# Four residual buffers instead of two, and a layernorm product written in place, in an eight-core random-feature and gated-FFN kernel

## The chip, the cores and the metric

The kernel runs on the 8 cores of one Trainium2 chip. Every core runs the same program on its own 2048 tokens, and nothing passes between the cores. The metric is the device time of one execution, in microseconds (us), taken on the slowest core. The profile is of core 1.

## The reference

For x of shape (4, 4096, 1024), 16384 tokens of width 1024:

```python
xn = _layernorm(x)
s = rfs_attention(xn)          # feats(xn) @ weights.T, both from exp(dot - correction)
h = silu(xn @ w1.T * w1_s) * (xn @ w2.T * w2_s)        # 1024 -> 4096
h = gelu(h @ h1.T * h1_s)                               # 4096 -> 4096
h = gelu(h @ h2.T * h2_s)                               # 4096 -> 4096
g = silu(h @ w3.T * w3_s)                               # 4096 -> 1024
x = x + s * g
```

## The kernel before

Each core works through its 2048 tokens in four sweeps of 512 (`for s_ in range(NS)`, L385). Activations lie feature-major: a tile of 128 features by 512 tokens is one matmul's moving operand. In a sweep TensorE (PE) does, in this order: `ffn1_strip` for 8 strips (L390 to L443: w1 at L401, w2 at L424), the layernorm broadcast of the next sweep (L273, L275), the two 4096 by 4096 layers h1 and h2 (L484), `emit_dot0` of the next sweep (L357), the w3 layer in two halves of four output tiles (L514), and `emit_smm` of the next sweep (L374). Sweep 0 does its own dot and smm product early; so there are three sweep boundaries at which the w3 half is followed directly by `emit_smm`, and one end of the program without it.

Weights come through `wring`, a ring of five slots of 1 MB in bf16 (2 MB in HBM, cast in flight), loaded by `ring_load` (L216, L222) on GpSimd's queue. A load waits until PE has used up the slot's last contents.

The residual part (L539 to L565) ends a sweep. The w3 output goes from PSUM through a Silu on ScalarE (L527) into `t2`, VectorE (DVE) multiplies it into `s_sb` (L534), adds x (L556, x being loaded by `xt_load` into a slot of `xt_r`), and SyncE (SP) stores `s_sb[:, dc, :]` to y (L562). There are eight tiles dc of 128 features in a sweep. `xt_r` has two slots, so the load of tile dc + 2 is issued only when the add of tile dc has freed its slot:

```python
for dc in range(8):
    slot = dc % 2
    ...
    av = V(... tensor_add(s_sb[:, dc, :], xt_r[:, slot, :], s_sb[:, dc, :]))
    if dc + 2 < 8:
        xt_load(dc + 2)
    need(sy, cV, av)
    sy.dma_start(y[...], s_sb[:, dc, :])
```

Waits are semaphore waits placed by `need`. Every engine runs its own program in the order in which the code emits it; no scheduler reorders it. What matters at a sweep boundary: `emit_smm` makes eight output tiles in PSUM banks 0 to 3, `oc % 4`. Its tiles 0 to 3 find their banks free. Tile 4 needs bank 0 again, so it waits for DVE to copy tile 0 into `s_sb` (L379). On DVE that copy is emitted behind the eight adds of L556. The copy also waits until the y store of the same `s_sb` tile has landed (`need(v, d_y[oc], ...)`, L378).

`ln2_bcast_affine` (L269 to L286) makes the normalised activations: for each of eight tiles a product into the fp32 tile `ln_tmp` (L280) and a subtraction into the bf16 tile `xn_fm` (L281), with the two PSUM banks 4 and 5 as second operands. In sweeps 1 to 3 it runs while PE is in h1; in sweep 0 PE waits for its last instruction (L282) before the first `emit_dot0`. Instructions of DVE are chained one behind the other by `V`, which waits for the instruction before.

Of the kernel before, what the change touches and what calls it, by code (L numbers as in the profile page):

```python
# [7 lines left out]
F32 = mybir.dt.float32  # L8
# [7 lines left out]
TS = 512  # L16
# [21 lines left out]
def build_nc():  # L38
    nc = bass.Bass("TRN2", target_bir_lowering=False)
    g = nc.gpsimd  # L40
    sy = nc.sync
    t = nc.tensor
    v = nc.vector
    sc = nc.scalar

    xT = nc.dram_tensor("xT", [D, T], F32, kind="ExternalInput").ap()
# [17 lines left out]
    with contextlib.ExitStack() as stack:  # L64
        E = stack.enter_context

        def sb(name, shape, dtype):
            return E(nc.sbuf_tensor(name, shape, dtype))
# [1 line left out]
        projT_sb = sb("projT_sb", [128, 9, R], BF16)  # L70
        Wt_sb = sb("Wt_sb", [128, 8, R], BF16)
        xt_sweep = sb("xt_sweep", [128, 8, TS], BF16)
        xt_r = sb("xt_r", [128, 2, 512], F32)
        rows = sb("rows", [128, 4, TS], F32)
        ln_tmp = sb("ln_tmp", [128, TS], F32)
        xn_fm = sb("xn_fm", [128, 9, TS], BF16)
        feats = sb("feats", [128, 8, TS], BF16)
        s_sb = sb("s_sb", [128, 8, TS], F32)
# [26 lines left out]
        p = [E(nc.psum_tensor(f"pb{i}", [128, 512], F32)) for i in range(8)]  # L105

        cT = Ctr(nc, stack, "cT", t)
        cV = Ctr(nc, stack, "cV", v)
        cS = Ctr(nc, stack, "cS", sc)
        d_xts = Ctr(nc, stack, "d_xts", g)  # L110
        d_xt = [Ctr(nc, stack, f"d_xt{i}", sy) for i in range(2)]
        d_y = [Ctr(nc, stack, f"d_y{i}", sy) for i in range(8)]
        d_wr = [Ctr(nc, stack, f"d_wr{i}", g) for i in range(5)]
        d_ident = Ctr(nc, stack, "d_ident", sy)
# [6 lines left out]
        def need(eng, ctr, val, allow_self=False):  # L121
            if ctr is None or val <= 0:
                return
            if ctr.eng is eng and not allow_self:
                return
            key = (id(eng), id(ctr.sem))
            if waited.get(key, 0) >= val:
                return
            eng.wait_ge(ctr.sem, val)
            waited[key] = val  # L130
# [3 lines left out]
        def guard_bank(i):  # L134
            gd = bank_guard.get(i)
            if gd is not None:
                need(t, gd[0], gd[1])

        def V(instr_fn):
            need(v, cV, cV.n, allow_self=True)  # L140
            return cV.inc(instr_fn())
# [74 lines left out]
        def ring_load(nm, strip, kk8, first):  # L216
            nonlocal ring_seq
            slot = ring_seq % 5
            fsrc = srcs[nm][strip] if nm in ("w1", "w2") \
                else srcs[nm][strip][:, kk8 * 8:(kk8 + 1) * 8, :]  # L220
            need(g, cT, slot_last[slot])
            g.dma_start(wring[:, slot, :, :], fsrc).then_inc(d_wr[slot].sem, 16)  # L222
            d_wr[slot].n += 16
            ring_seq += 1
            return slot, d_wr[slot], d_wr[slot].n
# [43 lines left out]
        def ln2_bcast_affine(s_, ffn1_last):  # L269
            need(t, cV, ln_state["rows"])  # L270
            guard_bank(4)
            guard_bank(5)
            bc1 = cT.inc(t.matmul(p[4][:, :], ones_row[0:1, :], rows[0:1, 2, :],  # L273
                                  start=True, stop=True))
            bc2 = cT.inc(t.matmul(p[5][:, :], ones_row[0:1, :], rows[0:1, 3, :],  # L275
                                  start=True, stop=True))
            need(v, cT, bc2)
            need(v, cT, ffn1_last)
            for j in range(8):
                V(lambda j=j: v.tensor_mul(ln_tmp[:, :], xt_sweep[:, j, :], p[4][:, :]))  # L280
                V(lambda j=j: v.tensor_sub(xn_fm[:, j, :], ln_tmp[:, :], p[5][:, :]))  # L281
            xr = V(lambda: v.tensor_copy(xn_fm[0:1, 8, :], rows[0:1, 1, :]))  # L282
            bank_guard[4] = (cV, xr)
            bank_guard[5] = (cV, xr)
            xts_state["guard"] = xr
            return xr  # L286
# [5 lines left out]
        xt_guard = {}  # L292
# [51 lines left out]
        ln2_stats(0)  # L344
        emit_wphase()
        xn_ready_sweep = ln2_bcast_affine(0, 0)

        def emit_dot0(xn_rdy):
            need(t, cast_sem["projT"], 16)
            need(t, cast_sem["xisrow"], 16)  # L350
            need(t, cV, xn_rdy)
            need(t, cV, cols_ready)
            for rc in range(8):
                bk = (6, 7, 4, 5)[rc % 4]
                guard_bank(bk)
                for j in range(9):
                    ii = t.matmul(p[bk][:, :], projT_sb[:, j, rc * 128:(rc + 1) * 128],  # L357
                                  xn_fm[:, j, :], start=(j == 0), stop=(j == 8))
                stop = cT.inc(ii)
                need(sc, cT, stop)  # L360
                ev = S(lambda rc=rc, bk=bk: sc.activation(
                    feats[:, rc, :], p[bk][:, :], AF.Exp,
                    bias=bias_f[:, rc:rc + 1], scale=ab_col[:, rc:rc + 1]))
                bank_guard[bk] = (cS, ev)
            return cS.n
# [19 lines left out]
        for s_ in range(NS):  # L385
            tok0 = s_ * TS
# [78 lines left out]
            if s_ + 1 < NS:  # L465
                xn_ready_sweep = ln2_bcast_affine(s_ + 1, ffn1_last)
# [3 lines left out]
            for nm, src_sb, dst_sb, s_col, src_rdy, dst_rec in (  # L470
# [3 lines left out]
                for ss in range(8):  # L474
# [3 lines left out]
                    for kk in range(4):  # L478
                        need(t, rdy_ctr, rdy_map[2 * kk + 1])
                        slot, wc, wv = ring_load(nm, ss, kk, s_ == 0)  # L480
# [19 lines left out]
            if s_ + 1 < NS:  # L500
                feats_next = emit_dot0(xn_ready_sweep)

            sg_done = [0] * 8
            for ss in range(2):
                quad = [0, 1, 2, 3] if ss == 0 else [4, 5, 2, 3]
# [2 lines left out]
                for kk in range(4):  # L508
                    need(t, cS, g2_by_strip[2 * kk + 1])
                    slot, wc, wv = ring_load("w3", ss, kk, s_ == 0)  # L510
# [11 lines left out]
                for og in range(4):  # L522
                    dc = ss * 4 + og
# [7 lines left out]
                for og in range(4):  # L531
                    dc = ss * 4 + og
# [3 lines left out]
                    t2_guard[og] = mv  # L536
                    sg_done[dc] = mv

            xt_val = {}  # L539

            def xt_load(dc):
                slot = dc % 2
                need(sy, cV, xt_guard.get(slot, 0))
                sy.dma_start(xt_r[:, slot, :],
                             xT[dc * 128:(dc + 1) * 128, tok0:tok0 + TS])\
                    .then_inc(d_xt[slot].sem, 16)
                d_xt[slot].n += 16
                xt_val[dc] = d_xt[slot].n

            xt_load(0)  # L550
            xt_load(1)
            for dc in range(8):
                slot = dc % 2
                need(v, cV, sg_done[dc])
                need(v, d_xt[slot], xt_val[dc])
                av = V(lambda dc=dc, slot=slot: v.tensor_add(  # L556
                    s_sb[:, dc, :], xt_r[:, slot, :], s_sb[:, dc, :]))
                xt_guard[slot] = av
                if dc + 2 < 8:
                    xt_load(dc + 2)  # L560
                need(sy, cV, av)
                sy.dma_start(y[dc * 128:(dc + 1) * 128, tok0:tok0 + TS],  # L562
                             s_sb[:, dc, :]).then_inc(d_y[dc].sem, 16)
                d_y[dc].n += 16
                y_val[dc] = d_y[dc].n  # L565
# [53 lines left out]
if __name__ == "__main__":  # L619
    nc = build_nc()  # L620
    print("built ok, instructions:", nc.n_instructions())
```

## Time and profile before

| what | value |
| --- | --- |
| median of 2 runs | 2897.07 us (2819.28 and 2974.87) |
| time of the profiled execution | 2818.11 us |
| its span, core 1 (first to last instruction) | 2816.4 us; the eight cores 2810.4 to 2816.4 |
| PE busy | 2636.4 us, 94% of the span |
| DVE, ACT, POOL busy | 251.3, 354.4, 205.3 us |
| mean granted TensorE clock | 0.976 |
| moved by DMA | 396.25 MB, mean 141 GB/s |

The profiled execution's own time is 1.7 us above its span. A row of the timeline is: start in us, duration in us, engine, line, operation, output<-input, count, and in brackets the idle time before it with what ended it. SPq is the SP engine's DMA issue. q0 is GpSimd's DMA queue (software), q1 is SP's (hardware). Idle time of an engine costs only where it delays the engine that sets the end.

### The profile page before, as it was taken

Reading aid. Unit: us, or ns where it says so; the run is one execution under the profiler, and the core shown is the slowest. Engines: PE = TensorE matmul, PEld = TensorE weight load, DVE = VectorE, ACT = ScalarE, POOL = GpSimd, SP = SyncE. Lnnn points to the kernel's source line nnn. Section 1 sums busy time; section 2 is a strip of 40 time slices with the busy share of each in tenths; the row PEclk is TensorE's granted clock in tenths of the full one; section 3 lists DMA queues with packets and bytes.
Section 4 is the critical chain, followed back from the end, with each engine's and each line's share of the span. In section 5 each row is a group of like instructions: output and inputs, shape, how many; then the busy total and the mean of one; then the engine's idle time right before and its main releaser. Section 6 shows DMA issues by size and latency. Waiting matters only on the chain.

```text
span 2816.4 us, 28223 instructions; the slowest of 8 cores (2810.4 to 2816.4 us)
## 1 busy us (share of the span) xinstructions
PE 2636.4 (94%) x12054; PEld 1184.5 (42%) x12054; DVE 251.3 (9%) x382; ACT 354.4 (13%) x493; POOL 205.3 (7%) x391
## 2 busy tenths in 40 slices
PE   2799999999879999999978999999987999999995
PEld 1344444444334444444433444444433444444442
DVE  2123000000022200000012310000002210000001
ACT  0211101010212110101101201010120110101100
POOL 1010000000000000000001000000000000000000
PEclk9899999999989999999998999999998999999997
DMA  9088888888569888888586988888865898888883
GB/s 157 2 137 139 156 152 151 153 154 153 94 134 164 148 151 151 152 153 154 107 141 121 158 152 153 154 153 150 151 117 121 148 153 153 155 153 151 152 154 75
DMA packets 67115, 396.25 MB, mean 141 GB/s; under 512 B 7328, under 2 KB 11696, under 8 KB 21936
## 3 DMA queue, kind: packets, MB, share of 16 engines
q0 software_dynamic: 57408, 377.51, 76.2%
q1 hardware_dynamic: 9584, 16.92, 2.3%
q8 instruction: 98, 1.61, 0.2%
q14 instruction: 25, 0.20, 0.0%
HBM read 763.51 MB, written 8.39 MB: 274 GB/s over the span
## 4 chain that ended last, share of the span: by engine, by line
PE 93%; DMA 3%; DVE 2%; ACT 1%; issue 1%; SPq 0%; DVEq 0%; POOL 0%; ACTq 0%
PE pb L484 63%; PE pb L514 8%; PE pb L401 8%; PE pb L424 8%; PE pb L357 2%; DMA xt_r<-xT 2%; PE pb L374 2%; DMA xt_sweep<-xT 1%; PE pb L333 1%; ACT t L527 0%; DVE s_sb L534 0%; DVE s_sb L556 0%; PE pb L243 0%; PE pb L245 0%; ACT h_sb L495 0%
## 5 line engine op out<-in xcount | busy, mean ns | idle before, releaser
L484 PE MATMUL pb<-h_sb,wring 128*128 128x512 bf16 x4096 | 884.7, 379 | 0.0
L484 PE MATMUL pb<-g_sb,wring 128*128 128x512 bf16 x4096 | 884.7, 379 | 0.0
L484 PEld LDWEIGHTS pb<-h_sb,wring 128*128 128x128 bf16 x4096 | 400.5, 98 | 484.8 <-issue 2.3
L484 PEld LDWEIGHTS pb<-g_sb,wring 128*128 128x128 bf16 x4096 | 400.8, 98 | 483.3
L514 PE MATMUL pb<-h_sb,wring 128*128 128x512 bf16 x1024 | 232.6, 391 | 18.8 <-ACT t L527 18.8
L401 PE MATMUL pb<-xn_fm,wring 128*128 128x512 bf16 x1024 | 231.5, 379 | 0.0
L424 PE MATMUL pb<-xn_fm,wring 128*128 128x512 bf16 x1024 | 231.4, 379 | 0.0
L534 DVE TENSOR_TENSOR s_sb<-t,s_sb 128x512 f32<-128x512 bf16 x32 | 22.2, 692 | 2028.2 <-ACT t L527 2025.4
L495 ACT ACTIVATE h_sb<-pb,h2s_c 128x512 bf16<-128x512 f32 x128 | 87.9, 687 | 795.8 <-PE pb L484 787.0
L495 ACT ACTIVATE g_sb<-pb,h1s_c 128x512 bf16<-128x512 f32 x128 | 87.9, 687 | 692.9 <-PE pb L484 683.7
L514 PEld LDWEIGHTS pb<-h_sb,wring 128*128 128x128 bf16 x1024 | 102.3, 100 | 148.4 <-issue 34.4
L424 PEld LDWEIGHTS pb<-xn_fm,wring 128*128 128x128 bf16 x1024 | 100.2, 98 | 120.8
L401 PEld LDWEIGHTS pb<-xn_fm,wring 128*128 128x128 bf16 x1024 | 99.9, 98 | 121.5 <-issue 1.3
L415 ACT ACTIVATE t<-pb,w1s_c 128x512 bf16<-128x512 f32 x128 | 87.9, 687 | 420.8 <-PE pb L401 414.8
L222 POOL DMA_DIRECT2D wring<-h1p x128 | 67.5, 528 | 827.6 <-PE pb L484 686.0
L222 POOL DMA_DIRECT2D wring<-h2p x128 | 67.5, 527 | 816.5 <-PE pb L484 816.5
L438 DVE SCALAR_TENSOR_TENSOR h_sb<-pb,w2s_c,t 128x512 bf16<-128x512 f32 x128 | 96.0, 750 | 336.5 <-PE pb L424 325.8
L374 PE MATMUL pb<-feats,Wt_sb 128*128 128x512 bf16 x256 | 64.2, 416 | 55.5 <-DVE s_sb L379 55.5
L357 PE MATMUL pb<-xn_fm,projT_sb 128*128 128x512 bf16 x288 | 66.8, 396 | 21.0 <-DVE xn_fm L282 13.4
L374 PEld LDWEIGHTS pb<-feats,Wt_sb 128*128 128x128 bf16 x256 | 26.7, 105 | 92.4 <-issue 67.4
L222 POOL DMA_DIRECT2D wring<-w2p x32 | 17.1, 535 | 530.7 <-PE pb L401 457.6
L357 PEld LDWEIGHTS pb<-xn_fm,projT_sb 128*128 128x128 bf16 x288 | 28.8, 101 | 59.4 <-issue 28.7
(71 smaller groups left out, 380.5 us busy)
## 6 DMA issues: line engine op xcount, KB each, us to landing
wring<-h1p POOLq DMA_DIRECT2D x128, 1024.0 KB, 8.2
wring<-h2p POOLq DMA_DIRECT2D x128, 1024.0 KB, 8.1
wring<-w1p POOLq DMA_DIRECT2D x32, 1024.0 KB, 11.9
wring<-w2p POOLq DMA_DIRECT2D x32, 1024.0 KB, 9.6
wring<-w3p POOLq DMA_DIRECT2D x32, 1024.0 KB, 8.0
xt_r<-xT SPq DMA_DIRECT2D x32, 256.0 KB, 4.6
y<-s_sb SPq DMA_DIRECT2D x32, 256.0 KB, 4.6
xt_sweep<-xT POOLq DMA_DIRECT2D x32, 128.0 KB, 11.8
```

The costliest lines, as they stand in the source:

```text
L222: g.dma_start(wring[:, slot, :, :], fsrc).then_inc(d_wr[slot].sem, 16)
L333: ii = t.matmul(p[bk][:, :], projT_sb[:, j, rc * 128:(rc + 1) * 128], iw_c[j][:, oh * 512:(oh + 1) * 512], start=(j == 0), stop=(j == 8))
L357: ii = t.matmul(p[bk][:, :], projT_sb[:, j, rc * 128:(rc + 1) * 128], xn_fm[:, j, :], start=(j == 0), stop=(j == 8))
L374: ii = t.matmul(p[bk][:, :], Wt_sb[:, rc, oc * 128:(oc + 1) * 128], feats[:, rc, :], start=(rc == 0), stop=(rc == 7))
L401: ii = t.matmul(p[ba1 + og][:, :], wring[:, slot1, k, (hh * 2 + og) * 128:(hh * 2 + og + 1) * 128], xn_fm[:, k, :], start=(k == 0), stop=( ...
L415: ev = S(lambda sl=sl, og=og, oc=oc, ba1=ba1: sc.activation(t1[:, sl, :], p[ba1 + og][:, :], AF.Silu, scale=w1s_c[:, oc:oc + 1]))
L424: ii = t.matmul(p[ba2 + og][:, :], wring[:, slot2, k, (hh * 2 + og) * 128:(hh * 2 + og + 1) * 128], xn_fm[:, k, :], start=(k == 0), stop=( ...
L438: ev = V(lambda oc=oc, og=og, sl=sl, ba2=ba2: v.scalar_tensor_tensor(h_sb[:, oc, :], p[ba2 + og][:, :], w2s_c[:, oc:oc + 1], t1[:, sl, :], ...
L484: ii = t.matmul(p[quad[og]][:, :], wring[:, slot, k8, og * 128:(og + 1) * 128], src_sb[:, kk * 8 + k8, :], start=(kk == 0 and k8 == 0), st ...
L495: sc.activation(dst_sb[:, oc, :], p[quad[og]][:, :], AF.Gelu, scale=s_col[:, oc:oc + 1]))
L514: ii = t.matmul(p[quad[og]][:, :], wring[:, slot, k8, og * 128:(og + 1) * 128], h_sb[:, kk * 8 + k8, :], start=(kk == 0 and k8 == 0), stop ...
L534: mv = V(lambda og=og, dc=dc: v.tensor_mul(s_sb[:, dc, :], t2[:, og, :], s_sb[:, dc, :]))
```

## The change

`xt_r` gets four slots instead of two, each with its own semaphore counter, and the load of tile dc + 4 follows the add of tile dc. The definition of `xt_load` and the first loads (now four) move up in the code, from behind the w3 layer to ahead of it. The fp32 tile `ln_tmp` (2 KB per partition) goes; the product of the layernorm is written as bf16 into its place in `xn_fm`, and the subtraction reads and writes it there. `xt_r` grows by 4 KB per partition.

```diff
-        xt_r = sb("xt_r", [128, 2, 512], F32)
+        xt_r = sb("xt_r", [128, 4, 512], F32)
         rows = sb("rows", [128, 4, TS], F32)
-        ln_tmp = sb("ln_tmp", [128, TS], F32)
...
-        d_xt = [Ctr(nc, stack, f"d_xt{i}", sy) for i in range(2)]
+        d_xt = [Ctr(nc, stack, f"d_xt{i}", sy) for i in range(4)]
...
             for j in range(8):
-                V(lambda j=j: v.tensor_mul(ln_tmp[:, :], xt_sweep[:, j, :], p[4][:, :]))
-                V(lambda j=j: v.tensor_sub(xn_fm[:, j, :], ln_tmp[:, :], p[5][:, :]))
+                V(lambda j=j: v.tensor_mul(xn_fm[:, j, :], xt_sweep[:, j, :], p[4][:, :]))
+                V(lambda j=j: v.tensor_sub(xn_fm[:, j, :], xn_fm[:, j, :], p[5][:, :]))
...
                 feats_next = emit_dot0(xn_ready_sweep)
 
+            xt_val = {}
+
+            def xt_load(dc):
+                slot = dc % 4
...
+            for dc in range(4):
+                xt_load(dc)
+
             sg_done = [0] * 8
...
-            xt_load(0)
-            xt_load(1)
             for dc in range(8):
-                slot = dc % 2
+                slot = dc % 4
                 need(v, cV, sg_done[dc])
                 need(v, d_xt[slot], xt_val[dc])
...
-                if dc + 2 < 8:
-                    xt_load(dc + 2)
+                if dc + 4 < 8:
+                    xt_load(dc + 4)
```

On PE, ScalarE, VectorE and GpSimd the instructions stand in the same order as before. SP's order changes. At the start of its program, before, behind the six small vector loads (`vec_sb`):

```order
L192 DMA vec_sb<-w3s 8x128
L544 DMA xt_r<-xT 128x512 x2
L544 DMA xt_r<-xT 128x512 [waits cV]
L562 DMA y<-s_sb 128x512
L544 DMA xt_r<-xT 128x512 [waits cV]
L562 DMA y<-s_sb 128x512
```

The same place now, where the loads' line is L507:

```order
L191 DMA vec_sb<-w3s 8x128
L507 DMA xt_r<-xT 128x512 x4
L507 DMA xt_r<-xT 128x512 [waits cV]
L562 DMA y<-s_sb 128x512
L507 DMA xt_r<-xT 128x512 [waits cV]
L562 DMA y<-s_sb 128x512
```

Two more loads are issued without a wait at the program's start. At the boundary of two sweeps SP's order before, where `cV` is DVE's counter, that is, the wait for an add:

```order
L544 DMA xt_r<-xT 128x512 [waits cV]
L562 DMA y<-s_sb 128x512
L544 DMA xt_r<-xT 128x512 [waits cV]
L562 DMA y<-s_sb 128x512
L562 DMA y<-s_sb 128x512 [waits cV] x2
L544 DMA xt_r<-xT 128x512 x2
L544 DMA xt_r<-xT 128x512 [waits cV]
L562 DMA y<-s_sb 128x512
```

And now:

```order
L507 DMA xt_r<-xT 128x512 [waits cV]
L562 DMA y<-s_sb 128x512
L507 DMA xt_r<-xT 128x512 [waits cV]
L562 DMA y<-s_sb 128x512
L562 DMA y<-s_sb 128x512 [waits cV] x4
L507 DMA xt_r<-xT 128x512 x4
L507 DMA xt_r<-xT 128x512 [waits cV]
L562 DMA y<-s_sb 128x512
```

In both kernels the first loads of a sweep stand directly behind the last y store of the sweep before, with no wait of their own; there are four of them now, and four loads instead of six that wait for an add.

## Rows read from the trace of the kernel before

**Rows 1.** The page, busy us of each engine (share of span) xinstructions.

```profile
PE 2636.4 (94%) x12054; PEld 1184.5 (42%) x12054; DVE 251.3 (9%) x382; ACT 354.4 (13%) x493; POOL 205.3 (7%) x391
```

**Rows 2.** Who waited for whom: us in total, times, longest us.

```profile
DVE s_sb L556 <- DMA xt_r<-xT: 58.2, 24, 7.2
PE pb L374 <- DVE s_sb L379: 57.3, 3, 20.3
...
PE pb L357 <- DVE xn_fm L282: 13.4, 1, 13.4
...
PE pb L424 <- DMA wring<-w2p: 0.9, 1, 0.9
```

**Rows 3.** Timeline of the first sweep boundary, 786 to 811 us.

```profile
786.46 0.53 POOL L222 DMA_DIRECT2D wring<-w1p  x1 [6.37 <-PE pb L514]
...
790.17 1.49 DVE L556 TENSOR_TENSOR s_sb<-xt_r,s_sb 128x512 f32<-128x512 f32 x2
790.95 0.33 SPq L544 DMA_DIRECT2D xt_r<-xT  x1
...
792.47 0.81 SPq L562 DMA_DIRECT2D y<-s_sb  x1
798.86 0.69 DVE L556 TENSOR_TENSOR s_sb<-xt_r,s_sb 128x512 f32<-128x512 f32 x1 [7.20 <-DMA xt_r<-xT]
...
800.12 0.69 DVE L556 TENSOR_TENSOR s_sb<-xt_r,s_sb 128x512 f32<-128x512 f32 x1 [0.57 <-DMA xt_r<-xT]
...
809.18 0.69 DVE L556 TENSOR_TENSOR s_sb<-xt_r,s_sb 128x512 f32<-128x512 f32 x1 [0.58 <-DMA xt_r<-xT]
...
810.81 9.41 PE L374 MATMUL pb<-feats,Wt_sb 128*128 128x512 bf16 x32 [17.99 <-DVE s_sb L379]
```

**Rows 4.** Timeline of the second sweep boundary: adds of tiles 3 and 7.

```profile
1475.20 0.69 DVE L556 TENSOR_TENSOR s_sb<-xt_r,s_sb 128x512 f32<-128x512 f32 x1 [0.64 <-DMA xt_r<-xT]
...
1487.21 0.69 DVE L556 TENSOR_TENSOR s_sb<-xt_r,s_sb 128x512 f32<-128x512 f32 x1 [1.78 <-DMA xt_r<-xT]
```

**Rows 5.** Timeline of the third sweep boundary: adds of tiles 3 and 7.

```profile
2154.75 0.69 DVE L556 TENSOR_TENSOR s_sb<-xt_r,s_sb 128x512 f32<-128x512 f32 x1 [0.64 <-DMA xt_r<-xT]
...
2165.49 0.69 DVE L556 TENSOR_TENSOR s_sb<-xt_r,s_sb 128x512 f32<-128x512 f32 x1 [2.41 <-DMA xt_r<-xT]
```

**Rows 6.** Timeline of the program's end: adds of tiles 3 and 7.

```profile
2800.72 0.69 DVE L556 TENSOR_TENSOR s_sb<-xt_r,s_sb 128x512 f32<-128x512 f32 x1 [0.47 <-DMA xt_r<-xT]
...
2812.14 0.69 DVE L556 TENSOR_TENSOR s_sb<-xt_r,s_sb 128x512 f32<-128x512 f32 x1 [2.37 <-DMA xt_r<-xT]
```

**Rows 7.** DMA queues, 791 to 796 us: packets, MB, share of 16 engines.

```profile
q0 software_dynamic: 92, 0.69, 90.6%
q1 hardware_dynamic: 21, 0.04, 11.0%
```

**Rows 8.** The same for 796 to 800 us.

```profile
q1 hardware_dynamic: 551, 1.00, 72.9%
```

**Rows 9.** Windows, 796 to 800 us; the last three: granted clock, DMA share, GB/s.

```profile
796.00:800.00 4.00, 0.00 (x0) 0.00 (x0) 0.69 (x1) 0.00 (x0) 0.00 (x0) 0.50 0.76 254
```

**Rows 10.** The page, DMA issues: count, KB each, median us to landing.

```profile
xt_r<-xT SPq DMA_DIRECT2D x32, 256.0 KB, 4.6
```

**Rows 11.** Groups of instructions by form: busy us, mean ns of one.

```profile
L438 DVE SCALAR_TENSOR_TENSOR h_sb<-pb,w2s_c,t 128x512 bf16<-128x512 f32 x128 | 96.0, 750 | 337.5 <-PE pb L424 326.7 <-ACT t L415 4.1
...
L280 DVE TENSOR_TENSOR ln_tmp<-xt_sweep,pb 128x512 f32<-128x512 bf16 x32 | 22.0, 688 | 39.3 <-PE pb L275 36.3
...
L234 DVE TENSOR_TENSOR feats<-xt_sweep 128x512 bf16<-128x512 bf16 x32 | 13.6, 425 | 4.9 <-DMA xt_sweep<-xT 1.7
```

**Rows 12.** Timeline of the program's start.

```profile
4.95 1.31 SPq L544 DMA_DIRECT2D xt_r<-xT  x2
...
44.08 4.13 DVE L234 TENSOR_TENSOR feats<-xt_sweep 128x512 bf16<-128x512 bf16 x8 [1.69 <-DMA xt_sweep<-xT]
```

**Rows 13.** The page, DMA queues: packets, MB, share of 16 engines over the span.

```profile
q1 hardware_dynamic: 9584, 16.92, 2.3%
```

More of the change, by code:

```diff
@@ L501, in build_nc @@
                 feats_next = emit_dot0(xn_ready_sweep)
+            xt_val = {}
+            def xt_load(dc):
+                slot = dc % 4
+                need(sy, cV, xt_guard.get(slot, 0))
+                sy.dma_start(xt_r[:, slot, :],
+                             xT[dc * 128:(dc + 1) * 128, tok0:tok0 + TS])\
+                    .then_inc(d_xt[slot].sem, 16)
+                d_xt[slot].n += 16
+                xt_val[dc] = d_xt[slot].n
+            for dc in range(4):
+                xt_load(dc)
             sg_done = [0] * 8
@@ L537, in build_nc @@
                     sg_done[dc] = mv
-            xt_val = {}
-            def xt_load(dc):
-                slot = dc % 2
[L543 to L548, printed above, removed]
-            xt_load(0)
-            xt_load(1)
             for dc in range(8):
-                slot = dc % 2
+                slot = dc % 4
                 need(v, cV, sg_done[dc])
```

## The prediction

> **What bounds the kernel now.** I read the page's first part before anything else: PE is busy 94% of the span [rows 1], so an edit pays only where PE stands still, or behind PE's last instruction. Then the view of who waited for whom. Two of its rows belong to this change: the residual adds wait 58.2 us for loads of `xt_r`, 24 times (six of eight in each of four sweeps), and PE waits 57.3 us in three stops for DVE's copy at L379 [rows 2]. The second is the first passed on: the copy that frees PSUM bank 0 stands on DVE behind all eight adds.
>
> The timeline of a sweep boundary shows how [rows 3]. DVE does adds 0 and 1 at once, from 790.17. Only then, at 790.95, can SP issue the third load, and add 2 starts at 798.86, 7.9 us later. Adds then come in pairs, each pair waiting for a fresh load; add 7 starts at 809.18, and PE goes on at 810.81 after a stop of 17.99 us. So a boundary pays three load latencies in a row, and so does the program's end, where add 7 is at 2812.14 [rows 6] and the span ends at 2816.4.
>
> The DMA queues tell why the first of them is long. From 791 to 796 us GpSimd's q0, still busy with the w1 load issued at 786.46, moved 0.69 MB and SP's q1 only 0.04 MB [rows 3, 7]. From 796 to 800 q1 moved 1.00 MB [rows 8]: two loads and two stores of 0.262 MB. SP's transfers in effect wait for the ring load to end, then go quickly.
>
> **The change, part by part.** *Hoisting the first loads.* SP's order shows that these stand directly behind the last store of the sweep before in both kernels; SP has nothing else to do meanwhile. Moving the code is worth nothing; the depth is what counts.
>
> *Four slots.* At a boundary four tiles are now in SBUF ahead of time. Adds 0 to 3 run from 790.17 without a wait, 0.79 us each, and the loads of tiles 4 to 7 follow them. The load of tile 4 takes the place that the load of tile 2 has now: issued at 790.95, behind the same ring load. So add 4 starts where add 2 starts now, 798.86, and add 5 where add 3 starts now, 800.12. Loads 6 and 7 stand right behind in the queue, each with one store ahead of it. The distance of adds 2 and 3, 1.26 us, is what one load and one store take when they queue like that. Two more such steps put add 7 at 800.12 + 2.52 = 802.64 in place of 809.18: **6.5 us** less.
> The same step at the other places, from add 3 to add 7 now: 1475.20 + 2.52 = 1477.72 for 1487.21, **9.5 us** [rows 4]; 2154.75 + 2.52 = 2157.27 for 2165.49, **8.2 us** [rows 5]; at the program's end 2800.72 + 2.52 = 2803.24 for 2812.14, **8.9 us** [rows 6]. What follows add 7 (the copy and PE's restart, or the last store) keeps its length. Sum 33.1 us.
> The 1.26 us is bounded from above by the mean rate over 796 to 800 us, 254 GB/s [rows 9]: a load and a store of 0.524 MB then take 2.06 us, and the four places lose 4 x 2 x 0.80 = 6.4 us, leaving 26.7. I take 1.26, because that stretch of 4 us holds the ramp and the tail of its transfers too.
>
> What is late next: loads 4 to 7. The stop shrinks from 18.0 to about 11.5 us and does not go. At its end the granted clock is 0.50 now, the lower level of 1.2 GHz [rows 9]; PE stopped at 792.8 and was already there in 796 to 800, before the new restart at about 804. So PE's first matmuls stay as slow, and I count no gain from the clock. The copy of tile 0 waits for its y store too: that store is one of the transfers that have landed by 800 [rows 8], ahead of the copy at about 803.4.
>
> The Trainium skill (DMA: Bandwidth & Descriptors, section Queues, rings and completion order) says that each DMA engine takes turns between the queues that have work, one packet at a time. Rows 7 have 92 packets of q0 beside 21 of q1, so the trace agrees in part at most. By the rule in full q1 would move 92 packets, about 0.17 MB, in those 5 us, 0.13 MB more, which at 254 GB/s is an estimated 0.5 us earlier at each boundary and 1.5 us in the sum.
>
> *Four loads at the start.* Before, SP issues two loads at 4.95 us, while q0 brings the weights and x; DVE still waits 1.69 us for the last of x before 44.08 [rows 12], and everything up to PE's first large product hangs on that. Two more loads are 0.524 MB. q1 moved 16.92 MB in 2.3% of 2816.4 us [rows 13], that is 64.8 us or 261 GB/s: **2.0 us** of all engines, taken from q0. Bounds 0 (if they fall into gaps) and 4 us (if each costs double while both queues are busy). I take 2.0.
>
> *The product in bf16, in place.* 16 instructions per sweep change their types and none is added or removed. The trace has no such form (bf16 out from bf16 and a PSUM operand in fp32). The nearest row is the product itself, 688 ns [rows 11]; a product with bf16 alone, without PSUM, takes 425 ns, and L438, bf16 out from PSUM with one operand more, 750 ns. In sweep 0, where PE waits 13.4 us for this chain [rows 2], that bounds it between 16 x 0.263 = 4.2 us less and 16 x 0.062 = 1.0 us more. I take 0, because one operand stays in PSUM. In the other sweeps h1 hides it: PE has no wait for L282 there (once in all [rows 2]).
>
> *Sum:* 33.1 - 2.0 = 31.1 us off the profiled execution's 2818.1 us: **2787 us**, 1.1% faster. The bounds of the terms give 26.7 - 4.0 - 1.0 = 21.7 to 33.1 + 4.2 + 1.5 = 38.8 us, 2779 to 2796. The profiled execution is 2.7% under the median of the two runs shown, 2897.07, and beside the lower of them, 2819.28; the forecast is for an execution like it.
>
> **Rivals.** *A second round trip stays (2795 us).* SP may not get loads 6 and 7 out before loads 4 and 5 have landed. For it: a fourth transfer in a row, the store at 792.47, took 0.81 us to issue in place of 0.33 [rows 3], so SP can be held up. Then each lands 4.6 us, the median [rows 10], behind loads 4 and 5: add 7 at 800.12 + 4.6 = 804.72. The gains are 4.5, 7.4, 6.1 and 6.8 us, 24.8 in all, 22.8 after the start. Against it: the hold was under a microsecond.
>
> *The first latency shrinks as well (2777 us).* If SP's transfers did not have to let the ring load end, load 4 would take the median 4.6 us in place of 7.9: 3.3 us more at each of three boundaries, 41 us in all. Against it stand rows 7: 0.04 MB in 5 us. The Trainium skill (the same page, section Anatomy of one DMA) fits a DMA at about 2.0 us plus its bytes at 436 GB/s, an estimated 2.6 us for such a load; by it the four places would gain another 2.0 us each, and the time would be about 2769 us. No load in the rows here is that quick.
>
> *The weight ring runs dry (2833 us, slower than before).* Place: the w1 and w2 products after a boundary. PE's long stop lets the ring fill; a shorter one, with 0.5 MB more of x loaded about then, could leave it short. One ring load of 1.05 MB at q0's 0.69 MB in 5 us [rows 7] takes 7.6 us; if two came late in each of three sweeps, that is 45.6 us, against 31.1 gained. It decides from 31.1 / 3 = 10.4 us per sweep, 1.4 loads. For it: PE did wait for a w2 load once, 0.9 us [rows 2]. Against it: the ring load of 786.46 had left the engines by 796, so the ring is full in the middle of the stop, and the prefetches go out at its end, when q0 has nothing to do until PE has used a strip.
>
> *The change does nothing at the boundaries (2820 us).* If what held the adds were not the loads, only the 2 us of the start would remain. The 24 waits of L556 all name a load [rows 2].
>
> **How the numbers follow.** Forecast 0.62, second round trip 0.20, shorter first latency 0.11, dry ring 0.04, nothing 0.03. The predicted time is 2787. The range takes in the bounds of the terms and the two faster rivals, down to 2768 and, for a second round trip together with a dear start, up to 2812; some 0.13 lies outside. A measurement of this kernel can tell about 2% from no change, 56 us: below 2762 lies little of the shorter latency (0.03), above 2874 little of the dry ring (0.03); within 2% 0.94.
>
> **What would show it.** Right: 16 waits of L556 for loads in place of 24, and adds 0 to 3 back to back, 0.79 us apart; three stops of PE before L374 of 11 to 12 us each; add 4 some 8 us behind add 0; the last add 4 to 5 us behind add 4; the chain at the start about 2 us later than now. Wrong: add 4 and add 6 each behind a wait of several us (a round trip stays), PE waiting for `wring` in L401 or L424 (dry ring), the layernorm's two operations away from 0.69 us, or stops of PE as long as now.

## The result and the profile after

The changed kernel takes 0.9911 of the time of the kernel before, 95% interval 0.9899 to 0.9922: 25 us less, 0.9%, where 31 us had been forecast. That is less than the 2% that a measurement of this kernel can tell from no change with certainty, but the interval lies wholly under 1. The median of 11 runs is 2795.05 us beside a forecast of 2787. (Medians can hold runs in which one die was disturbed and slower; ratios and comparisons leave these out, and without them the changed kernel took 2791.9 to 2795.5 us.)

The page of the changed kernel, busy time, then who waited for whom, on its slowest core (core 0); the lines answer to [rows 1] and [rows 2]:

```profile
PE 2634.8 (94%) x12054; PEld 1184.2 (42%) x12054; DVE 251.3 (9%) x382; ACT 354.5 (13%) x493; POOL 206.2 (7%) x391
```

```profile
PE pb L373 <- DVE s_sb L378: 38.6, 3, 13.0
...
DVE s_sb L556 <- DMA xt_r<-xT: 30.6, 16, 5.0
...
PE pb L356 <- DVE xn_fm L281: 13.4, 1, 13.4
```

The adds now wait 16 times in place of 24, as the forecast said, and 30.6 us in place of 58.2. PE's three stops are 38.6 us on this core in place of 57.3 on the profiled core before. The layernorm wait is the same 13.4 us.

The timeline of the first sweep boundary on core 1, the core of [rows 3]:

```profile
790.81 0.53 POOL L221 DMA_DIRECT2D wring<-w1p  x1 [6.37 <-PE pb L527]
...
794.51 3.08 DVE L556 TENSOR_TENSOR s_sb<-xt_r,s_sb 128x512 f32<-128x512 f32 x4
795.29 0.33 SPq L507 DMA_DIRECT2D xt_r<-xT  x1
...
797.22 1.42 SPq L507 DMA_DIRECT2D xt_r<-xT  x1
...
799.46 0.61 SPq L507 DMA_DIRECT2D xt_r<-xT  x1
...
801.54 0.69 DVE L556 TENSOR_TENSOR s_sb<-xt_r,s_sb 128x512 f32<-128x512 f32 x1 [3.95 <-DMA xt_r<-xT]
803.67 0.69 DVE L556 TENSOR_TENSOR s_sb<-xt_r,s_sb 128x512 f32<-128x512 f32 x1 [1.44 <-DMA xt_r<-xT]
805.01 0.69 DVE L556 TENSOR_TENSOR s_sb<-xt_r,s_sb 128x512 f32<-128x512 f32 x1 [0.65 <-DMA xt_r<-xT]
806.48 0.69 DVE L556 TENSOR_TENSOR s_sb<-xt_r,s_sb 128x512 f32<-128x512 f32 x1 [0.77 <-DMA xt_r<-xT]
...
808.11 9.57 PE L373 MATMUL pb<-feats,Wt_sb 128*128 128x512 bf16 x32 [10.94 <-DVE s_sb L378]
```

The reader is to see one latency where there were three: four adds in one row (3.08 us), 3.95 us of waiting, and then four adds as their loads come in. The stop is 10.94 us; it was 17.99.

The cores differ by some us, so the steps of the forecast are compared as means over the eight cores, each core read from its own timeline:

| step | before, us | after, us | measured | forecast |
| --- | --- | --- | --- | --- |
| three stops of PE ahead of L374 (now L373) | 55.4 | 34.9 | -20.5 | -24.2 |
| 96 matmuls behind the stops | 27.9 | 27.7 | -0.2 | 0 |
| PE's last matmul to the end of the last add | 22.2 | 14.6 | -7.6 | -8.9 |
| start of the last layernorm instruction of sweep 0 | 110.7 | 114.5 | +3.8 | +2.0 |
| sum | | | -24.5 | -31.1 |
| span | 2813.5 | 2788.8 | -24.7 | |

The sum of the steps, 24.5 us, is the change of the span, 24.7 us. Every step has the sign that was forecast and none is missing; three are off by 1 to 4 us.

The metric goes by the slowest core, and in this execution that is another core. Core 1, the profiled core before, went from 2816.4 to 2789.1 us. Core 0 ends last now, with 2793.9 us (other executions end with other cores): its layernorm ends late (the last instruction starts at 117.2 us, the mean is 114.5) and its stops are the longest (38.6 us, the mean is 34.9). The profiled execution, 2795.5 us, missed the forecast by 8.5 us: 6.4 of them are the steps of the table, 2.1 this spread of the cores.

### The profile page after: what moved, and what is told of

The parts are those of the page before. It is cut to its first block, busy times and chain, and to the rows that moved or that the text cites. A ratio compares the mean times of both kernels' runs of the same rounds, so it can differ in the third digit from the quotient of the medians.

```text
span 2793.9 us, 28223 instructions; the slowest of 8 cores (2783.7 to 2793.9 us)
## 1 busy us (share of the span) xinstructions
PE 2634.8 (94%) x12054; PEld 1184.2 (42%) x12054; DVE 251.3 (9%) x382; ACT 354.5 (13%) x493; POOL 206.2 (7%) x391
## 4 chain that ended last, share of the span: by engine, by line
PE 93%; DMA 3%; DVE 2%; ACT 1%; issue 1%; SPq 0%; DVEq 0%; POOL 0%; ACTq 0%
PE pb L483 63%; PE pb L527 8%; PE pb L400 8%; PE pb L423 8%; PE pb L356 2%; DMA xt_sweep<-xT 1%; PE pb L373 1%; PE pb L332 1%; DMA xt_r<-xT 1%; ACT t L540 0%; DVE s_sb L547 0%; PE pb L242 0%; PE pb L244 0%; DVE s_sb L556 0%; ACT h_sb L494 0%
## 5 line engine op out<-in xcount | busy, mean ns | idle before, releaser
L373 PE MATMUL pb<-feats,Wt_sb 128*128 128x512 bf16 x256 | 62.3, 406 | 38.6 <-DVE s_sb L378 38.6
L356 PE MATMUL pb<-xn_fm,projT_sb 128*128 128x512 bf16 x288 | 65.6, 391 | 21.0 <-DVE xn_fm L281 13.4
L242 PE MATMUL pb<-xt_sweep,ones_b 128*1 128x512 bf16 x32 | 14.8, 464 | 46.5 <-DVE feats L233 40.5
L373 PEld LDWEIGHTS pb<-feats,Wt_sb 128*128 128x128 bf16 x256 | 26.2, 103 | 74.1 <-issue 48.0
```

What stands on the lines that cost most here:

```text
L373: ii = t.matmul(p[bk][:, :], Wt_sb[:, rc, oc * 128:(oc + 1) * 128], feats[:, rc, :], start=(rc == 0), stop=(rc == 7))
```

## The experiments

Seven kernels were run. Times are given as the ratio to the kernel before, steps as means over the eight cores of the profiled execution. The kernel before was run again beside them and was some 4 us faster than beside the changed kernel (2815 to 2816 us, not 2819), so times in us are not compared with the changed kernel's that closely; ratios and steps are.

**No load of x at the start** (late_start).

```diff
+            if s_ == 0:
+                need(sy, cT, ffn1_last)
             for dc in range(4):
                 xt_load(dc)
```

> The changed kernel, but in sweep 0 the four first loads of x wait until PE has finished the w1 and w2 products of that sweep, so none is in flight at the program's start. In the changed kernel's profile the last layernorm instruction of sweep 0 (the cast, L281) starts at 114.5 us as a mean over the cores, before at 110.7. Theory, the two extra loads at the start cost this 3.8 us, 1.9 us each, on the path to PE's first product: with none the cast starts at 107 to 109 us, and the time is 2788 to 2790 us. Rival, the 3.8 us are a difference between two executions: the cast stays between 110 and 115 us and the time at 2795 within 2 us. The three stops of PE before L373 stay at 11 to 12 us in both.

Ratio 0.9902 (0.9880 to 0.9925), median 2787.54 us. The stops are the same, 35.3 us in all. The cast starts at 108.0 us in the mean. On core 1 of the changed kernel and then of this one (timeline; the issue of the first loads, and the cast):

```profile
4.46 2.86 SPq L507 DMA_DIRECT2D xt_r<-xT  x4
...
114.45 0.42 DVE L281 CAST xn_fm<-rows 1x512 bf16<-1x512 f32 x1
```

```profile
259.56 1.93 SPq L507 DMA_DIRECT2D xt_r<-xT  x4
```

```profile
108.78 0.42 DVE L281 CAST xn_fm<-rows 1x512 bf16<-1x512 f32 x1
```

The four loads cost 6.5 us of PE's start in these two executions, and holding them back loses nothing: they have the whole of h1 and h2, some 440 us, to land in. The timed ratio alone would not separate this kernel from the changed one (0.9902 and 0.9911, 2.5 us apart, and the intervals overlap); the cast does.

**More loads at the start** (more_at_start): eight loads of x tiles that nothing uses, so only their traffic counts.

```diff
+        for dc in range(8):
+            sy.dma_start(s_sb[:, dc, :], xT[dc * 128:(dc + 1) * 128, TS:2 * TS])\
+                .then_inc(d_dum.sem, 16)
...
+                need(v, d_dum, d_dum.n)
                 need(v, d_y[oc], y_val.get(oc, 0))
```

> The changed kernel with eight more loads of x tiles (256 KB each) at the start of SP's program, into s_sb, where nothing uses them. Casts at L281 so far as means over the cores: 108.0 us with no load at the start (late_start, split_adds), 110.7 and 111.4 with two (kernel before, ln_in_place_only), 114.5 and 113.0 with four (changed kernel, hold_ring): about 1.45 us per load. Theory, this price holds: the cast comes at about 125 us and the time is about 2807 us. Rival, the 261 GB/s of the forecast (1.0 us per load): 122 us and 2803 us. Rival, the queue of SP gets so little of the engines beside the ring's that more loads there hardly delay it: cast under 117 us, 2797 us.

Ratio 0.9953 (0.9934 to 0.9973), median 2804.21 us. The cast starts at 123.4 us in the mean; core 0 of this kernel (issue, x in SBUF, cast):

```profile
4.83 5.47 SPq L196 DMA_DIRECT2D s_sb<-xT  x8
...
57.01 4.13 DVE L238 TENSOR_TENSOR feats<-xt_sweep 128x512 bf16<-128x512 bf16 x8 [1.62 <-DMA xt_sweep<-xT]
...
123.45 0.41 DVE L286 CAST xn_fm<-rows 1x512 bf16<-1x512 f32 x1
```

DVE has the last of x at 57.0, where [rows 12] had 44.1. With all the runs, the mean cast by the number of loads at the start is: none 108.1 (three kernels), two 111.0 (three kernels), four 113.8 (two), twelve 123.4. From none to two, four and twelve that is 1.5, 1.4 and 1.3 us per load. The cast at 123.4 us misses the 125 of the theory and the 122 of the first rival by about the same, and the time, 2803 to 2804 us, is the rival's 2803: the loads beyond the fourth cost 1.2 us each, between the theory's 1.45 and the forecast's 1.0. The rival that SP's loads are all but free there is out. Two more loads are worth 113.8 - 111.0 = 2.8 us; the 3.8 us of the table hold a difference between executions besides.

**The layernorm edit alone** (ln_in_place_only).

```diff
-                V(lambda j=j: v.tensor_mul(ln_tmp[:, :], xt_sweep[:, j, :], p[4][:, :]))
-                V(lambda j=j: v.tensor_sub(xn_fm[:, j, :], ln_tmp[:, :], p[5][:, :]))
+                V(lambda j=j: v.tensor_mul(xn_fm[:, j, :], xt_sweep[:, j, :], p[4][:, :]))
+                V(lambda j=j: v.tensor_sub(xn_fm[:, j, :], xn_fm[:, j, :], p[5][:, :]))
```

> The kernel before with the layernorm product written in bf16 into xn_fm and ln_tmp left unused; two slots as before. Theory, as predicted: no cost, both DVE operations at 0.69 us, 2819 us within 3 us. Rival, the in-place form (or the bf16 product) costs part of what the forecast missed: 2825 us or more, or an operation away from 0.69 us. Second rival, the bf16 form runs faster, as the 425 ns product without PSUM does: 2815 us.

Ratio 1.0001 (0.9987 to 1.0016). Groups by form (busy us, mean ns of one):

```profile
L280 DVE TENSOR_TENSOR xn_fm<-xt_sweep,pb 128x512 bf16<-128x512 bf16 x32 | 22.0, 687 | 40.1 <-PE pb L275 37.1
...
L281 DVE TENSOR_TENSOR xn_fm<-xn_fm,pb 128x512 bf16<-128x512 bf16 x32 | 22.0, 687 | 3.3
```

687 ns each, where the product into fp32 took 688 [rows 11]. Both rivals are out; this part of the change is worth nothing in time and frees 2 KB per partition.

**The ring load held back** (hold_ring).

```diff
+                if ss == 2 and s_ > 0:
+                    need(g, cV, add_last)
                 slot1, wc1, wv1 = ring_load("w1", ss, 0, s_ == 0)
...
                 xt_guard[slot] = av
+                add_last = av
```

> The changed kernel, but the fifth ring load of sweeps 1 to 3 (w1 of strip 2, now issued just ahead of the adds) waits until the last add of the sweep before is done. Theory, SP's loads at a boundary wait for this ring load on the DMA engines: without it add 4 starts 4.5 to 5.5 us behind add 0 in place of 7 to 8, each stop of PE shrinks by 2 to 3 us to about 9, and the time is 2786 to 2789 us. Rival, the long first latency is that of SP's own four loads and four stores: add 4 and the stops stay as they are, 2795 us within 2 us. The w1 load then lands long before strip 2 needs it, so PE should not wait for the ring in either.

Ratio 0.9897 (0.9868 to 0.9926); its slowest core's span is 2783.5 us, the changed kernel's 2793.9. The first boundary on core 1:

```profile
792.25 3.08 DVE L558 TENSOR_TENSOR s_sb<-xt_r,s_sb 128x512 f32<-128x512 f32 x4
...
796.48 0.69 DVE L558 TENSOR_TENSOR s_sb<-xt_r,s_sb 128x512 f32<-128x512 f32 x1 [1.15 <-DMA xt_r<-xT]
...
802.76 0.53 POOL L221 DMA_DIRECT2D wring<-w1p  x1 [20.59 <-DVE s_sb L558]
803.11 9.21 PE L373 MATMUL pb<-feats,Wt_sb 128*128 128x512 bf16 x32 [8.20 <-DVE s_sb L378]
```

Add 4 starts 4.2 us behind add 0 here, 7.0 in the changed kernel. As means over the cores: 4.9, 5.1 and 4.8 us at the three boundaries, where the changed kernel has 7.1, 8.3 and 7.8; the stops are 8.9 us each, not 11.6. At the program's end, where no ring load is about, the changed kernel has 4.6 us. The theory holds in both numbers. By the ratios this kernel gains 4 us on the changed one, in intervals that overlap; by the mean spans of the profiled executions it is 10.9 us, of which 8.3 are the stops. One core of eight saw PE wait 1.0 us for the ring, which had not been expected; the kernel before has one such wait of 0.9 us [rows 2].

**The adds split** (split_adds): with the late first loads.

```diff
                     t2_guard[og] = mv
                     sg_done[dc] = mv
-
-            for dc in range(8):
-                slot = dc % 4
+                for dc in range(ss * 4, ss * 4 + 4):
+                    slot = dc % 4
...
```

> The changed kernel with the late first loads of late_start, and the adds of tiles 0 to 3 moved on DVE from behind the second half of w3 to behind the multiplications of the first half, so that loads 4 to 7 and stores 0 to 3 run under the second half. Theory, what is left of the stop is the latency of loads 4 to 7: the stop falls from 11.6 us (mean of 8 cores and 3 boundaries) to 1 to 2 us (four multiplications, four adds, one copy against four smm tiles of PE); a stop that short leaves TensorE at its upper clock, so the 32 matmuls after it take 6.9 in place of 9.4 us; the last add stands 7 us behind PE's last matmul in place of 14. Sum: 3 x 10 + 3 x 2.5 + 7 + 5 (start) = 49 us under the changed kernel, about 2746 us. Rival, the weight ring runs dry when the stop is gone: waits of PE for wring after each boundary, 2765 us or more.

Ratio 0.9755 (0.9733 to 0.9778), median 2746.73 us. The first boundary on core 1:

```profile
753.24 3.08 DVE L557 TENSOR_TENSOR s_sb<-xt_r,s_sb 128x512 f32<-128x512 f32 x4
...
787.27 3.08 DVE L557 TENSOR_TENSOR s_sb<-xt_r,s_sb 128x512 f32<-128x512 f32 x4
790.45 3.08 DVE L378 COPY s_sb<-pb 128x512 f32<-128x512 f32 x4
791.29 7.07 PE L373 MATMUL pb<-feats,Wt_sb 128*128 128x512 bf16 x32 [1.36 <-DVE s_sb L378]
```

The two blocks of adds stand 34 us apart, and the loads of tiles 4 to 7 land between them, unseen. The stop is 1.36 us, on all cores and at all boundaries within 0.01, and the 32 matmuls behind it take 7.07 us in place of 9.57, at a granted clock of 1.00 from 791.3 to 798.3 us. The last add ends 7.3 us behind PE's last matmul. The dry ring did not come: one core of eight waited 1.1 us for it, once. This version beats both kernels, by 2.4% and 1.6%.

The time came out as worked out, 2746.7 us for 2746, but partly by luck. Against the changed kernel the steps gain 30.8 us of stops, 6.5 us in the matmuls behind them, 7.3 us at the end and 6.5 us at the start: 51.1 us, where 49 had been worked out. The mean span fell by 46.0 us only. Some 4.5 us of the rest are lost at two places that nobody had counted on. In every sweep but the last PE waits 2.0 to 2.2 us for DVE ahead of the next sweep's layernorm sums (L242), and 2.5 us for ScalarE ahead of `emit_dot0` (L356), in all these kernels. In sweeps 1 and 2 all 16 groups of matmuls behind the first wait take 3.6 us in the changed kernel; here 15 of the 16 take 5.3 us. Behind the second wait one group of 24 takes 17.1 us in place of 15.7 in the changed kernel, and eight here. On core 4, the first wait of sweep 1 and a stretch behind it (the third number from the end is the granted clock), here and then in the kernel eight_buffers, told below:

```profile
1541.41 0.38 PE L242 MATMUL pb<-xt_sweep,ones_b 128*1 128x512 bf16 x1 [2.21 <-DVE h_sb L437]
...
1543.00:1546.00 3.00, 3.00 (x8) 0.88 (x7) 0.00 (x0) 0.00 (x0) 0.00 (x0) 0.50 1.00 191
```

```profile
1552.17 0.38 PE L246 MATMUL pb<-xt_sweep,ones_b 128*1 128x512 bf16 x1 [2.21 <-DVE h_sb L441]
...
1552.17:1555.70 3.53, 3.53 (x16) 1.25 (x16) 0.00 (x0) 0.00 (x0) 0.00 (x0) 1.00 1.05 188
```

The wait is the same, the clock behind it is not. What makes the difference is not shown.

**The adds split, with two slots** (split_two_slots): the kernel before but for the order of the adds; the first two loads move up in the code too, which leaves SP's order as it was.

```diff
-            for dc in range(8):
-                slot = dc % 2
+                for dc in range(ss * 4, ss * 4 + 4):
+                    slot = dc % 2
...
```

> The kernel before in everything (two slots, ln_tmp, two loads at the start) but the order of the adds: those of tiles 0 to 3 stand on DVE behind the multiplications of the first half of w3, as in split_adds. Theory, a boundary costs one load latency for every round of loads that is left behind the last multiplication: with two slots tiles 4 and 5 are then there ahead of time and only loads 6 and 7 are late, so add 7 takes the place that add 3 has in the kernel before. The stops fall from 18.5 to about 9.4 us each, the tail from PE's last matmul to the last add from 22.2 to about 11 us: 39 us less, 2780 us, better than the changed kernel with its four slots. Rival, the depth is what counts: no better than the changed kernel, 2795 us or more.

Ratio 0.9858 (0.9834 to 0.9882), median 2776.74 us. The stops are 8.6 us in the mean, the tail 11.1. Core 1, first boundary:

```profile
791.35 1.49 DVE L556 TENSOR_TENSOR s_sb<-xt_r,s_sb 128x512 f32<-128x512 f32 x2
...
799.76 0.69 DVE L556 TENSOR_TENSOR s_sb<-xt_r,s_sb 128x512 f32<-128x512 f32 x1 [6.92 <-DMA xt_r<-xT]
801.10 0.69 DVE L556 TENSOR_TENSOR s_sb<-xt_r,s_sb 128x512 f32<-128x512 f32 x1 [0.65 <-DMA xt_r<-xT]
...
802.74 9.87 PE L374 MATMUL pb<-feats,Wt_sb 128*128 128x512 bf16 x32 [8.73 <-DVE s_sb L379]
```

What counts is how many rounds of loads stand behind the last multiplication: three before, one in the changed kernel, one here with two loads in it, none in split_adds. The order of the adds alone, with no byte of SBUF, gives more than the change's two extra slots.

**Eight buffers** (eight_buffers): the other way to take the loads out of the stop.

```diff
+        xt_hi = g1_sb.ap().bitcast(F32).rearrange("p a b -> p (a b)")[:, 8192 - 2048:8192]
+        xt_buf = [xt_r[:, i, :] for i in range(4)] + \
+            [xt_hi[:, i * 512:(i + 1) * 512] for i in range(4)]
...
-            for dc in range(4):
+            need(sy, cT, h2_last)
+            for dc in range(8):
                 xt_load(dc)
```

> The changed kernel with eight buffers for x in place of four (four more in a part of g1_sb that is idle there), all eight loads of a sweep issued when h2 is done; order of the adds as in the changed kernel. No add waits for a load, and none is in flight at the start. Theory: the stop is DVE's own chain, four multiplications, eight adds and a copy: 1.36 us (split_adds) plus four adds of 0.79 us, 4.5 us. A stop of 4.7 us ahead of L514 in the kernel before leaves the first matmuls slow, so the 32 matmuls behind the stop take 9 to 9.6 us as now. Time: 2747 + 3 x 3.2 + 3 x 2.4 + 3.2 for the tail = 2767 us. Rival on the clock: it holds through 4.5 us of rest, the 32 matmuls take 7.07 us, and the time is 2760 us. Rival on the loads: eight loads beside the w3 ring loads come late, stops of 8 us or more.

Ratio 0.9806 (0.9787 to 0.9825). Who waited for whom on core 4, and on core 0:

```profile
PE pb L377 <- DVE s_sb L382: 13.6, 3, 4.5
```

```profile
PE pb L377 <- DVE s_sb L382: 15.3, 3, 5.2
...
DVE s_sb L382 <- DMA y<-s_sb: 2.3, 4, 0.7
```

No add waits for a load on either core. On cores 4 and 6 the stop is the 4.5 us that was worked out; on the others it is up to 6.5 us, because the copy of tile 0 now stands so close behind add 0 that it waits for the y store of the same tile: the next wait in line. And the clock did not hold: on core 4 the granted clock is 0.50 from 795.7 to 799.7 us, and the 32 matmuls behind the 4.54 us stop take 9.36 us.

```profile
795.71 9.36 PE L377 MATMUL pb<-feats,Wt_sb 128*128 128x512 bf16 x32 [4.54 <-DVE s_sb L382]
```

The time, 2761 to 2763 us, is some 5 us under the theory's 2767 and near the clock rival's 2760, though the clock did what the theory said. The 2767 was worked out from split_adds' time, which holds the 4.5 us lost at the two later places; here every group of sweeps 1 and 2 there takes 3.6 and 15.7 us.

## Why the prediction was right, and where its terms were off

*The mechanism.* Right in its parts. Hoisting moved nothing; the depth took away two of three latencies at each boundary and at the end (16 waits of L556, four adds in one row). The time alone does not say so: 2795 us is what the forecast had written beside its rival of a second round trip, and it lies just inside the slow end of the range that the bounds of the terms gave (2796). The steps below tell the two apart. Undone or pushed further, it follows: more of the waits away gives more (eight_buffers, split_adds), and the same result comes from order in place of depth (split_two_slots).

*"Add 5 where add 3 starts now."* Add 3 of the kernel before starts 9.2, 8.7 and 8.5 us behind add 0 (means at the three boundaries) and 6.2 at the end; add 5 of the changed kernel 9.2, 9.8, 9.7 and 6.4. Right at the first boundary and the end, 1.1 us short at the second and 1.2 at the third. On core 1, from which the forecast was read, it is right within 0.8 us at all three (9.2, 9.4 and 9.4 us, where add 3 had 9.95, 9.3 and 9.35).

*"Two more such steps of 1.26 us."* This term was mis-sized. From add 5 to add 7 the changed kernel takes 3.0, 3.0, 3.2 and 3.3 us, so 1.5 to 1.65 us a step and 0.5 to 0.8 us more than 2.52 at each place. One distance between two adds, at one boundary of one core, was too good a sample: 1.26 us for 0.524 MB is 416 GB/s. On core 1 itself the two steps took 2.8, 2.5 and 2.5 us at the boundaries, so there the term held; the mean of the cores and the end are slower. With eight transfers in a row q1's mean was 372 GB/s from 801 to 806 us on core 1, and 276 GB/s in the first 5 us of hold_ring, 794 to 799 us, which hold the ramp (349 GB/s from 797 to 802):

```profile
DMA packets 1024, 1.86 MB, mean 372 GB/s; under 512 B 115, under 2 KB 115, under 8 KB 1024
```

```profile
DMA packets 753, 1.38 MB, mean 276 GB/s; under 512 B 80, under 2 KB 80, under 8 KB 753
```

The bound of 2.06 us held in the means, though not on core 0 (2.2 us); the middle of the two ends, 1.66 us, would have been nearer. The profiled core before was also the one with the longest stops, 57.3 us against a mean of 55.4, so its gains could not be the mean's: on that same core the stops fell by 57.3 - 32.6 = 24.7 us, and the forecast from its rows was 24.2. Who waited for whom on core 1 of the changed kernel:

```profile
PE pb L373 <- DVE s_sb L378: 32.6, 3, 10.9
```

*The start.* 2.8 us by all runs, 3.8 in the profile shown, 2.0 forecast; inside its bounds. The rate of q1 over the whole span was taken for a stretch in which q0 is busy as well; that this is why it was too low is likely, not shown.

*The layernorm.* 0 as forecast (ratio 1.0001).

*The long first latency.* The forecast laid it to the ring load, from [rows 7] and [rows 8]; hold_ring shows it: 2.2 to 3.2 us at each boundary are that wait. The queues on core 0 of the changed kernel say the same, from 797 to 802 us, beginning a us before SP issued its load at 798.3:

```profile
DMA packets 106, 0.87 MB, mean 174 GB/s; under 512 B 0, under 2 KB 0, under 8 KB 0
...
q0 software_dynamic: 106, 0.87, 101.2%
```

There is no row of q1: SP's queue moved nothing in these 5 us. Its first packets stand in 802 to 803 us, 38 beside the last 18 of q0's load. The Trainium skill's rule that an engine takes turns between its queues packet by packet (DMA: Bandwidth & Descriptors, section Queues, rings and completion order) would have had q1 in this stretch; the measurement decides, though it is not shown that the profile's packets are the page's. An early start of the load gains little while the ring's is running. Part of the silence is the way from the issue to the first byte, which in hold_ring, with nothing in the way, kept q1 empty as well for about 1 us.

*The rivals.* The second round trip did not stay as a rule: from add 5 to add 7 there are 3.0 to 3.3 us in the means and from add 4 to add 6 2.7 to 3.6, where a round trip of its own would have taken 4.6. On core 0 it nearly did: add 7 comes 4.4 to 4.5 us behind add 5 at all three boundaries, and that core sets the time of this execution. SP was held up, as the rival had it: the issue of load 6 took 1.42 us on core 1, and that of load 7 took 1.58 us on core 0 at the first boundary. Whether the hold made the late add, and why it was core 0, no run shows. The first latency did not shrink by itself (a load of x takes 6.1 us in the median now, 4.6 before); it does when the ring load is held (hold_ring). The fit behind the 2.6 us of that rival stands in the Trainium skill (DMA: Bandwidth & Descriptors, section Anatomy of one DMA) for DMAs that GpSimd issues, not SP; no run here shows it for SP's loads. The ring did not run dry, neither here nor in split_adds, where the stop is all but gone. No run varied the number of tiles of w3 per half or the ring's depth.

## What to carry to other kernels

Count the rounds of latency that stand between the last producer and the instruction for which the busy engine waits, and ask of each whether order can hide it before buying buffers: moving half of the adds ahead of the last product gave 40 us with no SBUF, and with four slots and late first loads 69 us. A prefetch at the program's start is not free where PE's first products wait for loads too (1.2 to 1.5 us per 256 KB here); issue it where nothing else is late. Take the pace of a queue from a stretch as long as the one that you forecast and from several cores, not from the distance of two neighbours on one; and when the time is that of the slowest core, allow for another core to be the slowest.

## What the runs showed of the hardware that was not expected

A stop of 1.36 us left the 32 matmuls behind it at 7.07 us, with a granted clock of 1.00, the upper level of 2.4 GHz; a stop of 4.54 us made them 9.36 us, with 0.50 in the first 4 us of them, about as much as the stops of 18 us before, 9.41 on the profiled core [rows 3]. Behind all stops of 4.5 us and more they take 8.4 to 10.0 us. So at the boundary the part of a stop that is worth most is its last few us: from 4.5 to 1.4 us PE gains 3.2 us of waiting and 2.3 us of clock.

The length of a stop does not settle it, though. The same wait of 2.0 to 2.2 us ahead of L242 left the clock up in the changed kernel in sweeps 1 and 2 (3.6 us) and brought it down in split_adds (5.3 us, granted clock 0.50); in sweep 0 it takes 5.3 us in both kernels. So split_adds gave back some 4.5 of the 6.5 us of clock that it had gained at the boundaries.

While GpSimd's 1 MB cast load was running, SP's queue moved next to nothing, 0.04 MB in 5 us [rows 7] or no packet at all, and afterwards up to 372 GB/s. About 1 us of such a silence is there without the ring load too (hold_ring). The two queues shared the engines far from evenly in these stretches; the reason is open.
